# Layer 0 attention: the scores of the second query tile as three products of rounded parts

## The reference, cut to what matters

```
q = rmsnorm(hidden_states @ Wq_a, q_norm_w) @ Wq_b
kv = rmsnorm(hidden_states @ Wkv_a, kv_norm_w) @ Wkv_b
scores = jnp.einsum('bqhd,bkhd->bhqk', qf, kf) * scale
scores = jnp.where(mask[None, None], scores, jnp.finfo(scores.dtype).min)
p = jax.nn.softmax(scores, axis=-1)
o = jnp.einsum('bhqk,bkhd->bqhd', p, v)
```

## Time and profile before

| what | value |
|---|---|
| median of 3 runs | 540.04 us (539.3 to 541.05) |
| the profiled execution, its own time | 537.99 us |
| its span in the profile | 535.8 us |
| TensorE busy | 501.2 us, 94% of the span |
| VectorE busy | 377.3 us, 70% |
| ScalarE busy | 338.9 us, 63% |
| GpSimd busy | 294.7 us, 55% |
| granted TensorE clock, mean | 0.975 of 2.4 GHz |

### The profile page before, as it was taken

How to read it: one execution, slowest core, us unless ns; L and a number is a source line. 1 busy time by engine, 2 the same in 40 slices (tenths; PEclk the granted TensorE clock), 3 DMA queues, 4 the chain that set the end, 5 groups by cost and what they waited for, 6 DMA issues and landing times.

```text
span 535.8 us, 10729 instructions
## 1 busy us (share of the span) xinstructions
PE 501.2 (94%) x3600; PEld 437.3 (82%) x3600; DVE 377.3 (70%) x825; ACT 338.9 (63%) x755; POOL 294.7 (55%) x291
## 2 busy tenths in 40 slices
PE   7989999999999998799975879999999999999995
PEld 6768888888888787588854778999999999999884
DVE  2589888888885356755555788779766986678656
ACT  4457777777776655444432588778766876686673
POOL 4746777677775226336560577677544665465330
PEclk8999999999999999799996989999999999999999
DMA  8917999970000292345575000000000000000001
GB/s 265 393 64 281 323 314 329 332 252 0 0 0 1 94 410 79 105 132 160 166 256 187 1 1 2 0 1 2 1 1 2 0 1 2 1 2 1 1 21 60
DMA packets 17613, 56.79 MB, mean 106 GB/s; under 512 B 2612, under 2 KB 12346, under 8 KB 15770
## 3 DMA queue, kind: packets, MB, share of 16 engines
q1 hardware_dynamic: 14816, 49.81, 27.1%
q0 software_dynamic: 2752, 6.40, 3.6%
HBM read 49.19 MB, written 28.45 MB: 145 GB/s over the span
## 4 chain that ended last, share of the span: by engine, by line
PE 77%; DVE 8%; ACT 5%; issue 4%; POOL 3%; DMA 3%; SPq 0%; DVEq 0%; POOLq 0%; ACTq 0%
PE bank L442 10%; PE bank L444 10%; PE bank L443 10%; PE bank L990 5%; PE bank L585 5%; PE bank L507 5%; PE bank L610 3%; PE bank L587 2%; PE bank L734 2%; PE bank L1007 2%; PE bank L719 2%; PE bank L721 2%; PE bank L720 2%; PE bank L621 2%; PE bank L701 2%
## 5 line engine op out<-in xcount | busy, mean ns | idle before, releaser
L1099 ACT ACTIVATE probs<-bank,neg_max,q_scale 128x256 f32<-128x256 f32 (+1 forms) x128 | 63.8, 508 | 38.4 <-DVE neg_max L1742 38.4
L1951 POOL TENSOR_TENSOR probs<-probs,inv_sum 128x512 f32<-128x512 f32 x64 | 51.6, 828 | 44.3 <-DVE inv_sum L1750 44.3
L1984 POOL TENSOR_TENSOR exps<-exps,tables 128x256 f32<-128x256 f32 x32 | 24.6, 769 | 71.8 <-ACT exps L1209 71.7
L1209 ACT ACTIVATE exps<-bank 128x768 f32<-128x768 f32 x32 | 25.9, 809 | 41.3 <-PE bank L701 41.3
L1971 POOL TENSOR_TENSOR swapped<-swapped,tables 128x512 f32<-128x512 f32 x32 | 43.1, 1350 | 10.0 <-ACT swapped L1130 9.8
L1565 DVE TENSOR_TENSOR q_lo<-q_sum,q_hi 128x512 fp32r<-128x512 f32 x32 | 27.2, 851 | 29.7 <-ACT q_hi L1163 29.5
L2084 POOL DMA_INDIRECT y_rows<-y_slot,dest x31 | 29.7, 959 | 29.9 <-issue 19.1
L1728 DVE TENSOR_TENSOR swapped<-bank,tables 32x512 f32<-32x512 f32 x64 | 44.4, 694 | 1.4
L1943 POOL TENSOR_TENSOR qT<-qT,swapped 128x512 f32<-128x512 f32 x32 | 40.8, 1276 | 7.1 <-DVE swapped L1728 7.1
L442 PE MATMUL bank<-x,wq_hi 128*128 128x256 f32 x128 | 38.5, 301 | 3.2 <-DVE q_sum L1552 3.2
L585 PE MATMUL bank<-keysT,qT 128*128 128x256 f32 x128 | 38.3, 381 | 0.0
(11 more groups left out here) (283 smaller groups left out, 1774.2 us busy)
## 6 DMA issues: line engine op xcount, KB each, us to landing
slots<-in_c_unused SPq DMA_DIRECT2D x20, 1036.0 KB, 36.4
gu_all<-in_gate_up SPq DMA_DIRECT2D x4, 1024.0 KB, 7.9
xg<-slots SPq DMA_DIRECT2D x31, 129.5 KB
wvo_raw<-in_wvo SPq DMA_DIRECT2D x1, 2560.0 KB, 20.8
dn_all<-in_down SPq DMA_DIRECT2D x1, 2048.0 KB, 7.7
wq_full<-in_Wq SPq DMA_DIRECT2D x1, 2048.0 KB
wo_raw<-in_Wo SPq DMA_DIRECT2D x1, 2048.0 KB
wqk_raw<-in_wqk SPq DMA_DIRECT2D x1, 1536.0 KB, 10.4
```

The lines of the kernel that those rows point to most:

```text
L1099: ins = act.activation(probs[:, par, h, c0:c1], bank[:, 2 * par + h, c0:c1], ACT.Exp, bias=neg_max[:, par, i:i + 1], scale=q_scale[:, b, t ...
L1951: ins = pool.tensor_tensor(some, some, inv, ALU.mult)
```

## The change

The product of L585 becomes three products of rounded parts. The keys' parts are made once, before the units: the high part by ScalarE in two copies, the low part by VectorE in two subtractions. The second query tile's parts are made for each unit, two units ahead: the high part by ScalarE at the end of its `body`, the low part by GpSimd after the addition of its `body`, both into `q_parts`, which has a place for each batch. The parts of units 0 and 1 are made before the units: ScalarE makes their high parts after the load of the table, and GpSimd puts a low part behind the additions of units 0 and 1. TensorE waits for `q_lo` of a unit as well as for `q_ready`. The first query tile's product (L587) and the mask's stay as they are.

Three semaphores (`q_scaled`, `wq_lo` and one count of `latents`) are merged with others, which frees two names for `q_hi` and `q_lo`.

```diff
+    with ExitStack() as second:
+        q_parts = sb("q_parts", [P, 2, B, 2, P], F32R, second)
...
-    keysT = sb("keysT", [P, G, B * T])
+    keysT = sb("keysT", [P, 2, B * T])
+    keysT_parts = sb("keysT_parts", [P, 2, B * T], F32R)
...
             if own:
                 eng.wait_ge(at["q_ready"], n + 1)
+                eng.wait_ge(at["q_lo"], n + 1)
...
-                    eng.matmul(dst[:, 0:T], q[:, P:T], keysT[:, 0, T * b:T * b + T],
-                               start=True, stop=False, skip_group_check=True)
+                    keys = slice(T * b, T * b + T)
+                    three_pass(eng, dst[:, 0:T], q_parts[:, 0, b, h, :], q_parts[:, 1, b, h, :],
+                               keysT_parts[:, 0, keys], keysT_parts[:, 1, keys], True, False)
...
-            eng.wait_ge(kv["wq_lo"], PAIRS)
+            eng.wait_ge(kv["kv_lo"], 2 + PAIRS)
...
-        pe.wait_ge(su["keysT_copied"], 2)
+        pe.wait_ge(su["keysT_copied"], 4)
+        pe.wait_ge(su["latents"], 3)
...
+    def second(p, b, more):
+        if b < 2:
+            return p, b + 2
+        return (p + 1, b - 2) if more else None
+
+    def second_tile(p, b):
+        return qT[:, :, T * b + P:T * b + T]
+
+    def act_second_hi(act, at, p, b):
+        act.wait_ge(at["q_ready"], 4 * p + b + 1)
+        act.activation(q_parts[:, 0, b, :, :], second_tile(p, b), ACT.Copy).then_inc(at["q_hi"], 1)
+
+    def pool_second_lo(pool, at, p, b):
+        m = 4 * p + b
+        pool.wait_ge(at["q_ready"], m + 1)
+        pool.wait_ge(at["q_hi"], m + 1)
+        pool.tensor_tensor(q_parts[:, 1, b, :, :], second_tile(p, b), raw(q_parts[:, 0, b, :, :]),
+                           ALU.subtract).then_inc(at["q_lo"], 1)
...
     def act_attention0(act, at):
...
+            if own and second(p, b, more):
+                act_second_hi(act, at, *second(p, b, more))
+        for b in range(2):
+            act_second_hi(act, at, 0, b)
         steps(act, body)
...
             act.activation(keysT[:, 0, 512 * j:512 * j + 512], bank[:, j, :], ACT.Copy).then_inc(su["keysT_copied"], 1)
+            act.activation(keysT_parts[:, 0, 512 * j:512 * j + 512], bank[:, j, :], ACT.Copy).then_inc(su["keysT_copied"], 1)
...
+        for j in range(2):
+            dve.wait_ge(su["keysT_copied"], 2 * j + 2)
+            some = slice(512 * j, 512 * j + 512)
+            dve.tensor_tensor(keysT_parts[:, 1, some], keysT[:, 0, some], raw(keysT_parts[:, 0, some]),
+                              ALU.subtract).then_inc(su["latents"], 1)
         dve_first_queries(dve, at0)
...
             if own and ahead(p, b, more):
                 pool_sin(pool, at, *ahead(p, b, more))
+            if own and second(p, b, more):
+                pool_second_lo(pool, at, *second(p, b, more))
...
         for b in range(B - 1):
             pool_sin(pool, at0, 0, b)
+            if b < 2:
+                pool_second_lo(pool, at0, 0, b)
         pool_attention0(pool, at0)
```

More of the change, by code:

```diff
@@ L292, in build @@
     su = sems("setup", "wa_hi wa_lo tok_done key_raw_done q_squared rms_step rms_var rms_sqrt key_steps "
-              "latents lat_done latT_hi_done latT_lo_done q_scaled keyT_done keysT_copied fold_done "
+              "latents lat_done latT_hi_done latT_lo_done keyT_done keysT_copied fold_done "
               "fold_scaled fold_T_done fold_q_copied fold_o_done fold_o_copied rope_cols warmed")
@@ L302, in build @@
               "xgT_done xgT_copied up_done silu_done act_ready actT_done actT_copied down_done y_copied dest_ready")
-    kv = sems("kv1", "kv_hi kv_lo w_hi wq_lo w_lo k_done swap_done cos_done sin_done k_summed "
+    kv = sems("kv1", "kv_hi kv_lo w_hi w_lo k_done swap_done cos_done sin_done k_summed "
               "k_hi k_lo v_done v_copied ones")
     ff = sems("ffn", "abs_done halved bwT_done bw_hi bw_lo")
-    at0 = sems("a0", "w_hi_done w_lo_done q_done cos_done sin_done q_ready scores_done exp_done inv_ready ctx_done "
+    at0 = sems("a0", "q_hi q_lo w_hi_done w_lo_done q_done cos_done sin_done q_ready scores_done exp_done inv_ready ctx_done "
                "ctx_copied max_step max_ready probs_ready probsT_done probsT_copied")
@@ L1332, in _ @@
         act.wait_ge(su["fold_q_copied"], 4)
-        act.wait_ge(su["q_scaled"], 2)
+        act.wait_ge(su["rms_var"], 4)
         act_attention0(act, at0)
@@ L1810, in _ @@
         inv = inv_dev[:, 0, :].rearrange("p (b t) -> p b t", t=2)
-        dve.tensor_scalar(q_scale[:], inv, scale, None, ALU.mult).then_inc(su["q_scaled"], 1)
-        dve.tensor_scalar(q_minus[:], inv, -scale, None, ALU.mult).then_inc(su["q_scaled"], 1)
+        dve.tensor_scalar(q_scale[:], inv, scale, None, ALU.mult).then_inc(su["rms_var"], 1)
+        dve.tensor_scalar(q_minus[:], inv, -scale, None, ALU.mult).then_inc(su["rms_var"], 1)
         dve.wait_ge(su["rms_step"], 4)
@@ L1818, in _ @@
         split_w_low(dve, at0, 0)
-        dve.wait_ge(su["q_scaled"], 2)
+        dve.wait_ge(su["rms_var"], 4)
+        for j in range(2):
[3 more added lines that the diff above has]
+                              ALU.subtract).then_inc(su["latents"], 1)
         dve_first_queries(dve, at0)
@@ L1898, in _ @@
             dve.tensor_tensor(chunk(wq_lo, i), chunk(wq_full, i), raw(chunk(wq_hi, i)),
-                              ALU.subtract).then_inc(kv["wq_lo"], 1)
+                              ALU.subtract).then_inc(kv["kv_lo"], 1)
         weights()
```

## The result

The changed kernel takes 552.8 us (551.46 to 553.21, 4 runs) beside 539.72 us of the kernel before on the same chip: ratio 1.0258, 95% interval 1.0217 to 1.0299. It is 13.1 us slower; 11 had been forecast. Its profiled execution took 551.46 us with a span of 549.5 us, beside 537.99 and 535.8.

The account below looks back on a forecast made before the run. TensorE, busy 94%, was taken as the bound before the change. Start +3.6, thirteen loops +8.1 and last units -0.3 gave +11.4 us, a median of 551 us; forecast 547 to 555 (0.62), stated range 539 to 556.

Parts of the forecast that it names:

- TensorE's saving: Second query tile's scores: three rounded products replace one, saving 0.155 us a unit, 5.0 us over 32 units.
- The loop of two units: Attention: scores wait for GpSimd's subtraction made two units earlier; 9.38 us for two units, +8.1 us over thirteen loops.
- Where `neg_max` falls: In unit n + 2 it could begin at 8.40 us, in GpSimd's addition, and is held until 9.38.
- the odd unit's N: Start of the odd unit's normalising on GpSimd, put at 6.53 us after the even unit's neg_max ends.
- the sentence on the price of the subtraction: GpSimd's subtraction: at 1.09 us instead of 0.61, neg_max still falls in the addition and is released at the same point.
- The start: Before unit 2: parts behind the table load and GpSimd's queue delay the scores by +3.6 us, bounds 2.5 to 4.2.
- the first rival: The loop holds TensorE but neg_max finds gaps: 8.48 us for two units, 539.7 us in all; chance 0.14.
- The last units: Units 28 to 31: GpSimd's addition and most subtractions fall away, 0.155 us a unit comes back twice, some -0.3 us.
- After the attention: What follows the attention moves back as a whole, with no time of its own gained or lost.
- The faster rival: Low parts are in time, TensorE stays the bound, gains 5.0 us: 535.0, or 538.7 with start not hidden; chance 0.12.
- The slowest: neg_max held by GpSimd's addition in every unit, 5.26 us each, together 566; with cases between, chance 0.12.
- The neighbour without holds: Loop holds TensorE, neg_max finds gaps: 4.24 us a unit, 539.7 us in all; chance 0.14.

Follow-up runs that it names:

- `old_no_weights`: The changed kernel with TensorE's old product (still waiting for the low part) and most of the query weights' low part left out: 552.6 us, ratio 1.0253.
- `lo_before_addition`: The changed kernel with GpSimd subtracting the low part of unit n + 2 ahead of the addition of unit n + 3: 542.8 us, ratio 1.0089.
- `all_placed`: The changed kernel with the low part ahead of the addition, weights' parts made two pairs ahead, old product for units 0 and 1: 533.8 us, ratio 0.9901.
- `all_placed_neg`: `all_placed` with neg_max made by ScalarE in two small instructions: 533.2 us, ratio 0.9896.
- `old_product`: The changed kernel with TensorE's old product for the second query tile, parts still made and low part waited for: 555.8 us, ratio 1.0311.

## Why the prediction was right, point by point

- **TensorE's saving** of 0.155 us a unit is right: a unit that waits for nothing takes 4.17 us after, 4.32 before. That at most 0.4 of 4.0 us of it is kept in the loops of the changed kernel is shown by `old_no_weights`. The Trainium skill (FP8 and Floating Point Precision, TensorE Precision Notes) counts four passes for a float32 product, by which three would save 0.216 a unit, an estimate by that page; the chain has 0.36 us for the three products from 110.51 to 110.87 and so keeps to the smaller number.
- **The loop of two units** over GpSimd's subtraction is right. It was forecast at 9.38 us and is 9.34, alternating steps of 4.02 to 4.13 and 5.26 to 5.28 us. `lo_before_addition` shows that it is the place of the subtraction, not its work.
- **Where `neg_max` falls** was mis-sized, without harm. I had it 1.87 us after the odd unit's N and held for 0.98; it came after 2.30 (108.81 - 106.51) and was held for 0.41. The subtraction takes 0.72 us and not 0.61; a first product after a wait takes 0.36 us of the chain and not 0.12, so the scores' latency is 2.70 and not 2.46. Both delays went into the hold, as the sentence on the price of the subtraction said. It follows that the hold isn't what makes the loop long; the latency around it is, by some 9.0 of 9.34. That the loop came out within 0.04 us is owed to the point of release, which was right; how I split it into latency and hold was wrong, and the two errors cancelled there. They would not have in the first rival: I priced its loop without holds at 8.48 us and 3.6 us less in all, where about 9.0 a loop would be some 3 us more.
- **The start** was the term most off: +4.9 for +3.6, beyond the 4.2 that I gave as its upper bound. Of the 1.3 us, 0.4 lay ahead of the change's first instruction (the keys' copy begins at 29.01 and not 28.57; a difference from one execution to another as far as anything shows). Another 0.4 came up to the end of the `neg_max` of unit 0, which was held as forecast, but until 43.59: two subtractions take 0.72 us each and not 0.61, and 0.13 to 0.14 us pass between the end of a copy on ScalarE and the subtraction that waits for it. From there to the scores of unit 2 it took 6.42 us and not 5.94. The normalising of unit 0 (46.38) begins 2.79 us after its `neg_max` and not 2.49, since its reciprocal (46.13) stands on VectorE behind a sine product that ends at 46.10, an order that the sum did not have; the subtraction and its signal take the rest. The keys' parts cost nothing, as forecast.
- **The last units** gave nothing instead of -0.3.
- **After the attention** +0.9 us where nothing was forecast. In the changed kernel TensorE's granted clock is 0.81 in the first expert products, where it was 1.00 before. The two lines are from the stretch of the changed kernel and the same one of the kernel before, 13 us earlier:

```profile
236.00:245.00 9.00, 6.38 (x28) 4.82 (x27) 3.57 (x16) 2.36 (x7) 0.00 (x0) 0.81 0.41 104
```

```profile
223.00:232.00 9.00, 7.46 (x47) 5.83 (x45) 4.56 (x18) 2.69 (x8) 0.00 (x0) 1.00 0.44 119
```

In the chain, four of these products in a row take 1.45 and 1.71 us in two steps after; the same two steps take 0.86 each before, so 1.4 us comes from there, and 0.5 is made up elsewhere:

```profile
239.53 1.45 PE bank L996 x4
...
241.41 1.71 PE bank L996 x4
```

The work and its order are the same, and the three products aren't what decides. The 124 expert products of L996 take 33.1 to 33.6 us in all in seven of the thirteen profiled executions of this document and 32.0 to 32.1 in the other six. `lo_before_addition` and `all_placed`, which have the three products, are among the six, and `all_placed_neg` is among the seven. What brings the lower clock there stays open.

The faster rival fell by the wait of 0.65 to 0.88 us in every second unit; it needed 3.31 us from the start of the normalising to the end of the subtraction, and that takes 3.53 (106.51 to 110.04). The slowest needed the odd unit's scores later by 0.87 us and didn't come about, though `old_product` shows how near it is: one product of 1.28 us more in the odd unit made a step of 5.90. The neighbour without holds (4.24 a unit) is not met: even with no hold a loop is about 9.0 by the estimate above, 4.5 a unit.

## What to carry to other kernels

A work item that is made "two units ahead" is only ahead if its place in the queue is: count what stands before it in its engine's order, and close the loop over the engines with the durations of the trace. Here two neighbouring instructions in the other order gave back 9 of 13 us with no work removed. When such a wait goes, look at the next item of the same queue at once (the weights' low part), and at the code ahead of the loop, where everything waits for its first turn.

The saving on the engine that bounds the kernel was worth next to nothing here until the loop around it had slack. Price the edit with its support placed well before you judge it: the same three products come with +13 us in one placing and with -5 us in the other, where units 0 and 1 keep the old product.

## What the runs showed of the hardware that was not expected

- A held `neg_max` (128x4, two inputs in SBUF) ends with the GpSimd product that holds it, and so takes up a delay ahead of it: with scores 0.155 us later in each unit the loops stayed at 9.35 us within 0.02 (121.57 and 121.75 us for 13).
- After a wait of 2.3 to 3.5 us on TensorE its granted clock was 0.50 for some 3 to 7 us in six of eight profiled executions, and 1.00 in the other two.
- A product on TensorE that begins after a wait takes 0.36 us of the chain, one in a stream 0.12.
- The subtraction with a result in float32r and 128x256 takes 0.72 us on GpSimd, a float32 product of that size by a broadcast operand 0.61.
- Two ScalarE instructions on 128x2 numbers take 0.48 us in all, three times the 0.16 of one VectorE instruction on 128x4.
